# Gathering ten of twelve neighbour slots for 124 of 128 partitions in a sparse graph attention

## The reference

```python
h = maximum(layernorm(x), 0)
s_i = h @ attn[:128]
s_j = h @ attn[128:]
e = leaky_relu(s_i + s_j.T, negative_slope=0.2)
e = e + where(adj > 0, 0, -1e9)
alpha = softmax(e, axis=1)
out = x + alpha @ h
```

## Time and profile before

| | |
|---|---|
| median of three runs | 822.02 us |
| lowest, highest | 819.04, 822.57 us |
| profiled execution: span from first to last instruction | 819.9 us |
| profiled execution: its time outside the span | not on the page |
| instructions | 6412 |
| busiest engine | VectorE, 615.3 us |
| DMA packets, bytes | 39719, 301.59 MB |
| HBM read, written | 303.76, 8.98 MB |

### The profile page before, as it was taken

One profiled execution on the slowest core, in us unless ns is written; L12 is line 12 of the kernel. 1 busy time (PEld: TensorE's weight loads), 2 busy tenths in 40 slices (PEclk: granted clock), 3 DMA queues, 4 the chain that ended last, 5 costly groups with the idle time before them and its releaser, 6 DMA issues.

```text
span 819.9 us, 6412 instructions
## 1 busy us (share of the span) xinstructions
PE 379.5 (46%) x1378; PEld 171.4 (21%) x1378; DVE 615.3 (75%) x2028; ACT 534.3 (65%) x410; POOL 505.0 (62%) x526
## 2 busy tenths in 40 slices
PE   1546334444444344344343434444434546653765
PEld 1322011111111011111111101111111215431654
DVE  6898298677768667797778666697689799897831
ACT  4975676676676666766766666676676677764620
POOL 6720777755457767665547677555557667655771
PEclk9776665555555555555555555655555556766768
DMA  8999999999999999999999999999999999981210
GB/s 341 402 411 415 392 404 408 406 414 413 409 407 410 408 405 410 406 410 410 412 406 407 408 406 407 411 410 413 412 413 409 408 411 407 409 348 43 53 37 4
DMA packets 39719, 301.59 MB, mean 368 GB/s; under 512 B 10682, under 2 KB 17149, under 8 KB 22272
## 3 DMA queue, kind: packets, MB, share of 16 engines
q1 hardware_dynamic: 24032, 277.04, 83.1%
q0 software_dynamic: 15360, 23.88, 8.5%
q10 hardware_dynamic: 288, 0.26, 0.1%
HBM read 303.76 MB, written 8.98 MB: 381 GB/s over the span
## 4 chain that ended last, share of the span: by engine, by line
DMA 76%; issue 11%; DVE 5%; ACT 4%; PE 3%; POOL 0%; DVEq 0%; ACTq 0%
DMA adj_ring<-in_adj_dram 75%; ACT sign_ring L613 3%; PE words L1442 2%; DVE one_hot L724 1%; ACT h_all L625 1%; PE words L1406 1%; DMA x_all<-in_x_dram 1%; PE words L1366 0%; DVE cand L769 0%; DVE adj_ring L1142 0%; DVE adj_ring L1138 0%; DVE adj_ring L1146 0%; PE words L1516 0%; POOL out_dram L562 0%; ACT terms L620 0%
## 5 line engine op out<-in xcount | busy, mean ns | idle before, releaser
L613 ACT ACTIVATE sign_ring<-adj_ring,half_neg 128x4096 fp8e3<-128x4096 int32 x128 | 474.9, 3710 | 217.1 <-DMA adj_ring<-in_adj_dram 215.4
L521 POOL DMA_INDIRECT near<-h_table,near_id x384 | 391.8, 1020 | 235.4 <-issue 122.8
L1366 PE MATMUL words<-sign_ring,pack_w 128*128 128x512 bf16 x512 | 225.2, 592 | 354.8 <-ACT sign_ring L613 354.8
L769 DVE MAX8 cand<-words 128x8 f32<-128x256 f32 x256 | 90.9, 417 | 115.4 <-PE words L1366 115.4
L1366 PEld LDWEIGHTS words<-sign_ring,pack_w 128*128 128x128 bf16 x512 | 55.0, 127 | 521.9 <-ACT sign_ring L613 451.6
L954 DVE TENSOR_REDUCE sums<-terms 128x128 f32<-128x1024 f32 x58 | 112.2, 1934 | 2.0
L532 POOL DMA_INDIRECT near_m<-h_table,id_m x64 | 64.5, 1008 | 19.5 <-issue 19.2
L949 DVE TENSOR_TENSOR terms<-near,weight 128x512 f32<-128x512 f32 (+1 forms) x87 | 73.4, 871 | 0.0
L1357 PE MATMUL words<-place,place_w 128*128 128x512 bf16 x128 | 62.1, 586 | 3.6 <-DVE key L861 3.6
L1392 PEld LDWEIGHTS listing<-cand,one_hot 128*128 128x128 f32 x128 | 33.6, 321 | 10.9 <-issue 7.7
L1347 PE MATMUL listing<-h_all 128*1 128x128 f32 x128 | 19.1, 322 | 22.8 <-ACT h_all L625 22.8
(11 more groups left out here) (271 smaller groups left out, 524.3 us busy)
## 6 DMA issues: line engine op xcount, KB each, us to landing
adj_ring<-in_adj_dram SPq DMA_DIRECT2D x128, 2048.0 KB, 24.6
near<-h_table,near_id POOLq DMA_INDIRECT x384, 6.4
h_table<-h_all POOLq DMA_DIRECT2D x4, 1056.0 KB, 14.7
x_all<-in_x_dram SPq DMA_DIRECT2D x4, 1024.0 KB, 9.4
out_dram<-x_all SPq DMA_DIRECT2D x30, 128.0 KB, 23.9
near_m<-h_table,id_m POOLq DMA_INDIRECT x64, 6.4
out_dram<-x_all ACTq DMA_DIRECT2D x2, 128.0 KB, 2.5
adj_ring<-h_table SPq DMA_DIRECT2D x1, 132.0 KB, 2.6
```

The lines of the kernel that those rows point to most:

```text
L521: pool.indirect_dma_start(out=near[:, p % RING, k, :], out_offset=None, in_=table, in_offset=bass.IndirectOffsetOnAxis(ap=near_id[:, p % I ...
L613: nc.scalar.activation(bytes_of, adj_ring[:, n % HALVES, :].rearrange("p (d r i) -> p d r i", r=2, i=WORDS), ACT.Sign, bias=half_neg[:, :] ...
L769: last = nc.vector.max(out=cand[:, p % 2, t % 2, 8 * q:8 * q + 8], in_=words[t % 3][:, q * PART:(q + 1) * PART])
L1366: last = nc.tensor.matmul(at[:, k * BANK:(k + 1) * BANK], pack_w[:, d, :], twins[:, o + k * BANK:o + (k + 1) * BANK], start=False, stop=(d ...
```

## The change

The gathers of slots 1 to 7 and 9 to 11 are issued for partitions 0 to 123 (`WIDE`), in all pairs but the last; slots 0 and 8 keep 128 partitions. The rows of the last four partitions so own one slot each: their `floor` and the limit `empty` are set to a value that no code reaches, and the term -17 of `curve` becomes a value for each partition (`too_many`), which marks their rows for a list as soon as they have more than one neighbour. There are six lists in place of four, closed after pairs 5, 10, 15, 20, 26 and 32, with room for 124 rows each. A list's 16 gathers are issued in three pairs (6, 5, 5) in place of four, for 124 partitions except for the last list, and it is mixed four pairs after it is closed. The store of a list is for 124 partitions.

```diff
+    WIDE = 124
+    ENDS = (5, 10, 15, 20, 26, 32)
+    STARTS = (0,) + ENDS[:-1]
+    LISTS = len(ENDS)
+    BARRED = float(2 ** 26)
...
-    DEEP_PARTS = (4, 4, 4, 4)
-    DEEP_MIX = 6
+    DEEP_PARTS = (6, 5, 5)
+    DEEP_MIX = 4
+    MIXED_LISTS = {ENDS[m] + DEEP_MIX: m for m in range(LISTS - 1)}
+    GATHERED_LISTS = {ENDS[m] + k: (m, k) for m in range(LISTS - 1) for k in range(len(DEEP_PARTS))}
...
+            nc.gpsimd.memset(empty[:, :], EMPTY)
+            nc.gpsimd.memset(too_many[:, :], -17.0)
...
+            for g in (0, 2):
+                nc.gpsimd.affine_select(out=floor[:, g, 1:OWN], in_=floor[:, g, 1:OWN], compare_op=ALU.is_gt,
+                                        fill=BARRED, base=WIDE, pattern=[[0, OWN - 1]], channel_multiplier=-1)
+            nc.gpsimd.affine_select(out=empty[:, :], in_=empty[:, :], compare_op=ALU.is_gt, fill=BARRED,
+                                    base=WIDE, pattern=[[0, 1]], channel_multiplier=-1)
+            nc.gpsimd.affine_select(out=too_many[:, :], in_=too_many[:, :], compare_op=ALU.is_gt,
+                                    fill=-17.0 - 2 * (2 * OWN - 1), base=WIDE, pattern=[[0, 1]], channel_multiplier=-1)
...
                 for k in range(SLOTS):
+                    rows = P if k in (0, 2 * OWN) or p == PAIRS - 1 else WIDE
                     pool.indirect_dma_start(
-                        out=near[:, p % RING, k, :], out_offset=None, in_=table,
-                        in_offset=bass.IndirectOffsetOnAxis(ap=near_id[:, p % IDS, k:k + 1], axis=0),
+                        out=near[0:rows, p % RING, k, :], out_offset=None, in_=table,
+                        in_offset=bass.IndirectOffsetOnAxis(ap=near_id[0:rows, p % IDS, k:k + 1], axis=0),
...
+                rows = WIDE if m < LISTS - 1 else P
                 for k in slots:
                     pool.indirect_dma_start(
-                        out=near_m[:, k, :], out_offset=None, in_=table,
-                        in_offset=bass.IndirectOffsetOnAxis(ap=id_m[:, k:k + 1], axis=0),
+                        out=near_m[0:rows, k, :], out_offset=None, in_=table,
+                        in_offset=bass.IndirectOffsetOnAxis(ap=id_m[0:rows, k:k + 1], axis=0),
...
-                if p >= SEG and p % SEG == DEEP_MIX:
-                    store_m(p // SEG - 1)
+                if p in MIXED_LISTS:
+                    store_m(MIXED_LISTS[p])
...
-                nc.vector.tensor_scalar(floor[:, 3::-2, ::-1], best[:, 1::2, :], EMPTY, None, ALU.max).then_inc(find, 1)
+                nc.vector.tensor_scalar(floor[:, 3::-2, ::-1], best[:, 1::2, :], empty[:, 0:1], None, ALU.max).then_inc(find, 1)
...
-                nc.vector.scalar_tensor_tensor(curve[:, :], excess[:, ts], -17.0, excess[:, ts], ALU.add, ALU.mult) \
+                nc.vector.scalar_tensor_tensor(curve[:, :], excess[:, ts], too_many[:, 0:1], excess[:, ts], ALU.add, ALU.mult) \
...
-                nc.vector.scalar_tensor_tensor(spilled[:, :], key[:, :], P - FAR, in_list[:, :], ALU.is_ge, ALU.mult) \
+                nc.vector.scalar_tensor_tensor(spilled[:, :], key[:, :], WIDE - FAR, in_list[:, :], ALU.is_ge, ALU.mult) \
...
-                dve.wait_ge(listed, SEG * m + SEG)
+                dve.wait_ge(listed, ENDS[m])
...
-                if m >= 0 and p % SEG == 0:
-                    find_deep(m)
+                if p in ENDS:
+                    find_deep(ENDS.index(p))
```

More of the change, by code:

```diff
@@ L52, in graph_attention_kernel @@
     OWN = 4
-    SEG = 8
-    SEGS = PAIRS // SEG
+    WIDE = 124
[3 more added lines that the diff above has]
+    BARRED = float(2 ** 26)
     DEEP = 16
@@ L138, in graph_attention_kernel @@
         floor = sb("floor", [P, 4, OWN], fp32)
+        empty = sb("empty", [P, 1], fp32)
+        too_many = sb("too_many", [P, 1], fp32)
         half_neg = sb("half_neg", [P, 1], fp32)
@@ L544, in store_m @@
                 for e in range(2):
-                    pool.wait_ge(stored[e], 16 * (m + 1) * SEG // 2)
+                    pool.wait_ge(stored[e], 16 * ((ENDS[m] + 1 - e) // 2))
                 pool.indirect_dma_start(
-                    out=out, out_offset=bass.IndirectOffsetOnAxis(ap=row_m[:, m % 2:m % 2 + 1], axis=0),
-                    in_=mixed_m[:, 0, :], in_offset=None,
+                    out=out, out_offset=bass.IndirectOffsetOnAxis(ap=row_m[0:WIDE, m % 2:m % 2 + 1], axis=0),
+                    in_=mixed_m[0:WIDE, 0, :], in_offset=None,
                     bounds_check=last_row, oob_is_err=False).then_inc(stored_m, 16)
@@ L572, in _ @@
                     load_lone(0)
[L573 to L577, removed]
+                if p in GATHERED_LISTS:
+                    m, k = GATHERED_LISTS[p]
+                    at = sum(DEEP_PARTS[:k])
+                    gather_m(m, range(at, at + DEEP_PARTS[k]))
+            gather_m(LISTS - 1, range(0, DEEP))
             load_lone(LAST)
@@ L594, in _ @@
                     pool.sem_inc(far_free, 1)
-            store_m(SEGS - 1)
+            store_m(LISTS - 1)
             store_lone(LAST)
-            pool.wait_ge(stored_m, 16 * SEGS)
+            pool.wait_ge(stored_m, 16 * LISTS)
             pool.wait_ge(lone_stored[0], 16)
@@ L681, in _ @@
                 sign_tile(2 * p + 1, (0,))
-                if p >= SEG and p % SEG == DEEP_MIX:
-                    exp_m(p // SEG - 1)
+                if p in MIXED_LISTS:
+                    exp_m(MIXED_LISTS[p])
                 sign_tile(2 * p + 1, (1,))
@@ L712, in _ @@
                     nc.scalar.activation(far_pt, far_u, ACT.Copy).then_inc(far_pt_ready, 1)
-            exp_m(SEGS - 1)
+            exp_m(LISTS - 1)
         @block.vector
@@ L848, in flag_pair @@
                     .then_inc(flagging, 1)
-                if p % SEG == 0:
+                if p in STARTS:
                     nc.vector.memset(prior[:, p % 2, 0:1], 0.0).then_inc(flagging, 1)
@@ L1231, in _ @@
                 mixes = MIXES.get(p, [])
-                m = p // SEG - 1
                 lone_begin(p)
@@ L1236, in _ @@
                     key_pair(p - 1)
-                if m >= 0 and p % SEG == DEEP_MIX:
-                    score_deep(m)
+                if p in MIXED_LISTS:
+                    score_deep(MIXED_LISTS[p])
                 for g in mixes:
                     score_pair(g)
-                if m >= 0 and p % SEG == DEEP_MIX:
-                    add_deep(m)
+                if p in MIXED_LISTS:
+                    add_deep(MIXED_LISTS[p])
                 max_tile(2 * p + 1)
@@ L1259, in _ @@
                     score_pair(BODY + 1)
-                    find_deep(SEGS - 1)
+                    find_deep(LISTS - 1)
                     weigh_pair(BODY + 1)
@@ L1331, in _ @@
                                                    ALU.mult, ALU.add).then_inc(far_out_ready, 1)
-            score_deep(SEGS - 1)
-            add_deep(SEGS - 1)
+            score_deep(LISTS - 1)
+            add_deep(LISTS - 1)
             lone_end(LAST)
@@ L1388, in list_pair @@
                 pe.wait_ge(hot_ready, 2 * p + 2)
-                if p % SEG == 0 and p > 0:
-                    pe.wait_ge(find_m, FIND_M * (p // SEG))
+                if p in STARTS and p > 0:
+                    pe.wait_ge(find_m, FIND_M * STARTS.index(p))
                 for a in range(2):
                     last = nc.tensor.matmul(listing[:, 0:REC], one_hot[:, p % 2, a, :], cand[:, p % 2, a, :],
-                                            start=(p % SEG == 0 and a == 0), stop=(p % SEG == SEG - 1 and a == 1))
+                                            start=(p in STARTS and a == 0), stop=(p + 1 in ENDS and a == 1))
                 last.then_inc(listed, 1)
```

## The result

The changed kernel takes **985.93 us** (median of four runs, 985.17 to 988.19) against 821.91 us before on the same chip (819.04 to 822.57): a ratio of 1.201, 95% interval 1.199 to 1.203. It is 164 us slower, where 808 us was forecast. The profiled execution took 985.44 us, its span is 983.7 us, so some 1.7 us lie around the span.

A forecast was written before the change was run, and what follows sets the result against it. The DMA engines were taken to bound the stream. Terms -16.0 + 0.8 + 0.3 + 0.5 = -14.4 us gave a span of 805.5 and a time of 808 us; range 802 to 828, likeliest case alone 802 to 814.

The forecast's parts named there:

- the first term: Narrow gathers in the stream: 124 rows go as four data pieces in place of 16, saving 16.0 us per engine.
- rival 1: No fewer pieces: 124 rows use all 16 engines, or shares of 31 are cut into eights; 825 us, chance 0.38.
- the 0.068 us a gather: Upper limit on every DMA engine's time per gather beyond its bytes; 0.056 given to the data piece, the rest to the completion.
- Rival 2: POOL becomes the bound above 1.16 us an issue; at 1.20 us some 840 us; chance 0.10, shared with DVE's overrun.
- The two lists: Two more lists: 32 more gathers +0.8 us per engine, more bytes +0.3 us, more instructions to fetch +0.5 us.
- DVE's extra work: Finding, mixing and scoring two more lists on DVE: 22 us, costed at nothing because DVE waits 115.4 us in the stream.
- The lower bound's 803.7 us: Low end of the likeliest case: all 0.068 us is the data piece's, 19.4 us saved; less 1.7 us gives 802.
- DVE's overrun in pairs 26 to 28: Finding a list there adds 3.3 us to a nearly full DVE; slower if beyond cover, chance 0.10 shared with rival 2.

The follow-up runs named there:

- lists_full_width: The changed kernel with every gather and list store issued for 128 partitions again: 825.55 us, ratio 1.0041 to the kernel before.
- delayed issues: The changed kernel with all gathers and list stores at 128 rows, two small GpSimd operations after each gather the change had narrowed: 926.35 us, ratio 1.1315.

## Why the prediction was wrong

**The step that failed is the first term**: "I take four", -16.0 us, a gain of 0.042 us for each of 380 gathers. The four shares of 31 were right. Each was then cut into four pieces of up to eight rows, which rival 1 had as its second way, so that a gather kept its 16 pieces with rows; and the twelve other engines got four empty pieces each, which neither the forecast nor a rival held. Per engine a gather went from one data piece and a completion to four and a completion. In place of -0.042 us it costs +0.28 us: the sum of the queues' shares, as engine time, gives

```
rows of the narrow gathers      packets    engines busy              idle
128 (lists_full_width)             32    91.9% of 823.3 = 756.6 us    66.7 us
112                                32    91.9% of 849.2 = 780.4       68.8
120                                32    92.0% of 862.3 = 793.3       69.0
126                                48    91.8% of 871.1 = 799.7       71.4
124 (the change)                   80    88.0% of 983.7 = 865.7      118.0
128, delayed issues (the last)     32    82.3% of 922.2 = 759.0      163.2
```

and (865.7 - 756.6) / 390 = 0.28 us. Of the 109 us, q1 has 58 (740.7 against 682.5) and q0 50 (122.0 against 71.6). Gathers of 112 rows bring 24 us and of 120 rows 37, with no packet more, which I put down to the straight shares; a second piece on each engine brings 6 us more (126); the four pieces with all that goes with them another 66.

**What an empty piece costs.** Counted over the trace's packets from 90 to 720 us, where one starts as another ends, a packet of adj takes 612 ns at the median when it follows another of adj, in the kernel before, and 613 in the changed one. In the changed kernel it takes 693 ns after an empty piece and 699 after one with rows; in the kernel before it was 668 after a piece with rows, and 615 after a completion. In the cases in which the packets of one engine can be followed so, at most one of q0 stands between two of adj in over nine of ten, in both kernels; over all, the changed kernel has 2.2 of q0 for one of adj, so elsewhere several follow each other. So each piece, empty or not, slows the packet behind it, a completion hardly, and a piece mostly waits for a turn of its own. The forecast took the 0.068 us a gather of the earlier trace rows as the price of a piece and a completion, which was right in kind; it then multiplied it by the wrong number.

**Rival 2 happened as well.** Its point was 1.16 us an issue, and 1.38 was measured. Its place and sign were right, and its price too small for that, since it had been worked out at 1.20 us (840 us). By its own sum at 1.38 us, five pairs take 66 x 1.68 + 12 x 1.31 = 127 us against 114, 64 us in all on top of 825; the delayed issues, at the same mean step, measured 104.

**The two loads meet, as I read it.** The engines' work alone would make 866 us and the 66 us that they are idle at the ends anyway, 932; GpSimd's pace alone some 930 (1.1315 x 822). The changed kernel takes 984, more than either. The trace shows where the rest lies. GpSimd stands still eight times between two gathers from 120 to 790 us, for 5.7 to 10.5 us, 69 us in all; its waits for DVE's near_id are 32 us, and the profile shows nothing for the others. With the delayed issues it never stood so before the stream's end, and the 57 us between the two kernels are of that size. Meanwhile DVE waits for near, and the engines stand idle 51 us more than in lists_full_width. That neither side covers the other's delays when both need nearly the same time is my reading; no run isolates it. Whether a fourth place in `near` would loosen this loop was not tried.

**What was right.** The two lists: +1.6 us forecast, or +3.0 in rival 1, and 3.4 measured; rival 1's 825 us is what the change costs at equal pieces, and its 16,512 packets are lists_full_width's to the packet. DVE's extra work: 22 us forecast, 20.6 measured there (635.9 us busy against 615.3), hidden but for what part it has in the 3.4 us. (The lower bound's 803.7 us comes out at some 804.0 by the forecast's own terms, which doesn't move the range.) That the stream was bound by the DMA engines, as the forecast had it, is why every extra piece could count. DVE's overrun in pairs 26 to 28 did not show as a cost beyond those 3.4 us either.

No version here beats the kernel before; lists_full_width, the best of the variants, is 0.4% slower.

## What to carry to other kernels

A transfer's cost on a full stream goes with its number of pieces on each engine, so count them for the new shape, empty ones too: 128 rows to 124 took a gather from 32 packets to 80. The count is not all of it, for even 112 rows, with 32 packets, cost 4%. Try one transfer of the new shape first: its packets and its issue time, 80 and 1.38 us here, would have warned of this result. And two resources that each come to the same time may cost more together than the larger of them, as here.

## What the runs showed of the hardware

- A gather of 112 rows, in 16 equal shares and 32 packets like one of 128, slows the stream from 407 to 390 GB/s; what differs, besides the rows left out, is that a share is seven consecutive partitions, not two groups of four.
- An issue takes GpSimd 1.00 us with 128 rows, 0.99 with 112, 1.07 with 120, 1.06 with 126 and 1.38 with 124 (medians). It does not follow the number of packets (32, 32, 32, 48, 80) evenly, and why is open.
- Of the 64 data pieces of a gather of 124 rows 48 move no row, and the packet of adj behind such a piece took 693 ns at the median in place of 613.
- Loading adj in packets of 8 KB in place of 16 made the kernel before 20% slower, and in the changed kernel the window with almost only adj moved 270 GB/s in place of 431, with the DMA engines no less full (share 0.99). This was not followed up.
